# A gated block with quantized feed-forward: PSUM copies for the low weight halves, a second buffer for turned z, the down product three tiles behind, and tile norms on ScalarE

## The chip, the cores and the metric

One core of a Trainium2 chip runs the whole program as one launch. The metric is device time in microseconds; lower is better. The kernel before takes 396.05 us (median of 3 runs, 395.64 to 396.24).

## The reference

There are 2048 tokens (4 x 512) of width D = 512. Two gated residual branches follow one another:

```python
x = x + tanh(g_xattn) * experts(layernorm(x), token_ids)   # 4 experts, picked by token id
x = x + tanh(g_ffn)   * ffn(layernorm(x))
# expert e:  g = silu(h @ W[e].T); u = h @ W[e].T; y = (g * u) @ W[e].T    (all three weights are ctx[e])
# ffn:       out = bit_linear(silu(bit_linear(x, gate)) * bit_linear(x, val), out)   (hidden width 2048)
# bit_linear: each row of x scaled by 127 / max|x| and rounded, weights rounded to -1, 0, 1 times mean|w|
```

## The kernel before

**Experts.** The tokens are sorted by expert on the chip and cut into 19 units of 128 rows (`UNITS`), each with one expert. A unit is gathered from memory (`gather` on GpSimd), normalised on VectorE (`unit_stats`, `norm`), turned on TensorE (`turn_h`), and multiplied with its expert's 512 x 512 weight by 12 matmuls in half precision: high x high, low x high and high x low parts (`product`, L501). ScalarE and VectorE make g * u (`silu`, `gu`), TensorE turns that and multiplies again with the same weight, and VectorE adds the result to the rows (`x1`). GpSimd then writes the rows to `x1_rows` in memory (`scatter`). The low part of the weights (`w_low`) is made once in eight pieces of 128 x 1024, six on VectorE (L812) and two on GpSimd (L364), from the loaded weights and their high part, both in SBUF. One `slot` of TensorE handles the first product of unit j and the second of unit j - 1. Meanwhile ScalarE sums the feed-forward weights' magnitudes (`sum_abs`), GpSimd rounds them (`round_pair`, L375) and ScalarE makes them ternary (`sign_pair`).

**Feed-forward.** The rows come back as 16 tiles of 128 (`load_rows`). Per tile VectorE applies the norm (`tile_norm`, L914, into the PSUM bank `xn`; GpSimd makes the reciprocal deviation, `tile_rstd`, L341) and finds the row maximum (`x_max`, L920); ScalarE rounds (`x_round`, `x_unshift`); a DMA turns the tile (`turn_x`). TensorE does two halves of the gate product and of the value product, 8 matmuls of 512 columns each (`gate`, `val`), and the down product, 2 x 8 matmuls into one bank `o_ps` (`down`, L576). VectorE scales the four results and adds biases (`pre_gate` L940, `pre_val` L948). ScalarE takes silu (L730). GpSimd multiplies the halves to z (`z_pair`, L416, 128 x 1024). VectorE finds z's maximum (`z_max`, L953) and, after a few small steps, its scale (`z_scales`, L967); ScalarE rounds z in two halves (`z_round`, L718); GpSimd takes the rounding constant off the first half (`unshift_z`, L410) and ScalarE off the second (L726); SyncE's queue issues the turns (`turn_z`) into the single buffer `ziT`. VectorE ends a tile with `finish` (L978), and GpSimd stores it (`store`, L429) after it had added a bias to the residual rows (`add_bias`, L423).

**What sets the order.** Each engine's program is written out by hand, and runs strictly in that order; semaphores tie the engines. In feed-forward slot t VectorE runs `pre_gate(t,0)`, `pre_val(t,0)`, `z_max(t-1,1)`, `tile_norm(t+2)`, `x_max(t+2)` among the small steps of tile t-1's scale, `pre_gate(t,1)`, `z_max(t,0)`, `pre_val(t,1)`, `finish(t-2)`. GpSimd runs `z_pair(t-1,1)`, in every second slot `tile_rstd`, `store(t-3)`, `add_bias(t+1)`, `unshift_z(t-1)`, `z_pair(t,0)`. ScalarE runs `silu_gate(t,0)`, both `z_round(t-1)`, `unshift_z(t-1)`, `silu_gate(t,1)`, `x_round(t+2)`, `x_unshift(t+2)`. TensorE does tile t's four products with `down(t-2)` between them; each down product waits for the `finish` before it.

## Time and profile before

| | before |
|---|---|
| median of 3 runs | 396.05 us (395.64 to 396.24) |
| the profiled execution | 394.75 us, of which 393.0 us are the profile's span |
| TensorE matmul busy | 314.2 us (80%) |
| VectorE busy | 275.3 us (70%) |
| GpSimd busy | 230.3 us (59%) |
| ScalarE busy | 199.8 us (51%) |
| mean granted TensorE clock | 0.947 of full |

The busy times are sums over stages with different limits. Positions in the span are microseconds from its start. The experts' last product ends at about 157.3 us, and the first matmul of the feed-forward runs at 151.5 us. On VectorE and ScalarE rows that follow one another overlap by some 0.1 us, so steps are counted from start to start.

### The profile page before, as it was taken

The page shows a single profiled execution, that of the slowest core. Times are in us where ns is not written, and L with a number is a line of the kernel's source. Part 1 is how long each engine was busy: PE and PEld are TensorE (multiplying, and loading weights), DVE is VectorE, ACT ScalarE, POOL GpSimd, SP SyncE. Part 2 cuts the span into 40 slices and gives each one's busy share as a digit, 9 for nine tenths or more (in the row PEclk, how much of TensorE's full clock was granted, in tenths as well). Part 3 has the DMA queues.
Part 4 walks back from the last instruction along what each step waited for, and adds up shares of the span by engine and source line. Part 5 has one row for each costly group of instructions (what it writes and reads, how often), then busy time and mean ns, then how long its engine had stood idle before and what let it go on. Part 6 is the DMA issues. An engine that isn't in the chain of part 4 may idle for free.

```text
span 393.0 us, 5131 instructions
## 1 busy us (share of the span) xinstructions
PE 314.2 (80%) x1421; PEld 145.6 (37%) x1438; DVE 275.3 (70%) x519; ACT 199.8 (51%) x247; POOL 230.3 (59%) x237
## 2 busy tenths in 40 slices
PE   2966999999999599867598689787986986897533
PEld 1332555455555244323143234233432432343110
DVE  5696877678987476678668766966796687666510
ACT  4723558687864365163663456355536634555200
POOL 2564446877884933475656657575766566566310
PEclk9999999999999989999899899899899898999676
DMA  7697576652327411214432532344244314331240
...
DMA packets 54612, 47.50 MB, mean 121 GB/s; under 512 B 46847, under 2 KB 46847, under 8 KB 52288
## 3 DMA queue, kind: packets, MB, share of 16 engines
...
q8 instruction: 9, 0.15, 0.2%
q14 instruction: 11, 0.09, 0.1%
...
## 4 chain that ended last, share of the span: by engine, by line
POOL 36%; issue 25%; DVE 15%; PE 12%; DMA 8%; ACT 1%; POOLq 1%; DVEq 1%; SPq 1%
POOL w_both L416 15%; PE banks L501 8%; DMA xg<-in_x,gather_at 5%; DVE raw L948 5%; POOL raw L423 5%; POOL w_both L410 5%; POOL out L429 4%; POOL raw L375 2%; PE banks L576 1%; DVE x_sb L851 1%; POOL raw L341 1%; DVE bn L856 1%; POOL var_eps L338 1%; POOL xg L316 1%; DMA raw<-x_rows 1%
## 5 line engine op out<-in xcount | busy, mean ns | idle before, releaser
L501 PE MATMUL banks<-w_both,turned 128*128 x456 | 106.8, 384 | 7.2 <-DVE w_both L812 2.8
L576 PE MATMUL banks<-tern,w_both 128*128 128x512 bf16 x255 | 71.1, 432 | 43.1 <-DVE raw L978 34.1
L416 POOL TENSOR_TENSOR w_both<-raw 128x1024 f32<-128x1024 f32 (+1 forms) x32 | 74.9, 2340 | 41.4 <-DVE raw L948 41.4
L953 DVE TENSOR_REDUCE raw<-w_both 128x1 f32<-128x1024 f32 x32 | 38.9, 1216 | 55.8 <-POOL w_both L416 55.8
L556 PE MATMUL banks<-tern,raw 128*128 128x512 bf16 x241 | 62.5, 394 | 4.3 <-DVE raw L948 2.5
L501 PEld LDWEIGHTS banks<-w_both,turned 128*128 128x128 f16 x456 | 44.9, 98 | 56.1 <-issue 13.6
L718 ACT ACTIVATE w_both<-w_both,magic,raw 128x1024 f32 (+1 forms) x32 | 38.0, 1233 | 52.8 <-DVE raw L967 52.8
L565 PE MATMUL banks<-tern,raw 128*128 128x512 bf16 x256 | 60.5, 379 | 2.2 <-DVE raw L940 2.2
L730 ACT ACTIVATE raw<-raw 128x1024 f32<-128x1024 f32 x32 | 33.6, 1049 | 53.3 <-DVE raw L940 53.3
L576 PEld LDWEIGHTS banks<-tern,w_both 128*128 128x128 bf16 x256 | 26.3, 107 | 83.4 <-issue 39.9
L329 POOL DMA_INDIRECT x_rows<-x_sb,scatter_at x19 | 20.4, 1072 | 42.2 <-DVE x_sb L861 40.8
L940 DVE SCALAR_TENSOR_TENSOR raw<-banks,raw 128x1024 f32<-128x1024 f32 x32 | 40.9, 1277 | 0.5
L948 DVE SCALAR_TENSOR_TENSOR raw<-banks,raw 128x1024 f32<-128x1024 f32 x32 | 40.8, 1275 | 0.0
L556 PEld LDWEIGHTS banks<-tern,raw 128*128 (+1 forms) x256 | 26.1, 103 | 38.3 <-issue 7.7
L565 PEld LDWEIGHTS banks<-tern,raw 128*128 (+1 forms) x256 | 24.8, 98 | 33.2 <-DVE raw L940 3.7
L410 POOL TENSOR_SCALAR w_both<-w_both,magic,one 128x1024 bf16<-128x1024 f32 x15 | 17.9, 1192 | 31.8 <-ACT w_both L718 31.8
L670 ACT ACTIVATE tern<-raw,magic 128x1024 bf16<-128x1024 f32 x24 | 26.9, 1146 | 12.0 <-POOL raw L375 12.0
L375 POOL TENSOR_SCALAR raw<-raw,inv_gam,magic 128x1024 f32<-128x1024 f32 x24 | 28.8, 1202 | 0.1
L429 POOL DMA_INDIRECT out<-raw x16 | 17.0, 1063 | 18.9 <-DVE raw L978 16.5
...
L828 DVE BATCH_NORM_STATS2 bn<-xg 128x6 f32<-128x512 f32 x19 | 13.0, 686 | 17.1 <-DMA xg<-in_x,gather_at 17.1
L664 ACT ACTIVATE tern<-raw 128x1024 bf16<-128x1024 f32 x21 | 22.1, 1051 | 0.1
...
## 6 DMA issues: line engine op xcount, KB each, us to landing
...
w_both<-w_both SPq DMA_TRANSPOSE x32, 3.2
```

The lines of the kernel that those rows point to most:

```text
L375: nc.gpsimd.tensor_scalar(w, w, inv_gam[:, m:m + 1], magic[:, 0:1], ALU.mult, ALU.add).then_inc(rounded, 1)
L410: nc.gpsimd.tensor_scalar(zi[:, 0:H // 2], zq[:, 0:H // 2], magic[:, 1:2], one[:, 0:1], ALU.add, ALU.mult).then_inc(zi_made[0], 1)
L416: nc.gpsimd.tensor_tensor(z[:, t % 2, 2 * D * c:2 * D * c + width], g_sb[:, c, 0:width], v_sb[:, c, 0:width], ALU.mult).then_inc(z_made, 1)
L501: last = nc.tensor.matmul(acc[:, :], a[:, k * P:(k + 1) * P], flat(w[:, bass.ds(e4 + k, 1), :]), start=(k == 0 and i == 0), stop=(k == KD ...
L556: last = nc.tensor.matmul(ring[pair][:, b, :], flat(xiT[:, bass.ds(t % 2, 1), k, :]), tern[:, k * HC + 2 * c + b, :], start=(k == 0), stop ...
L565: last = nc.tensor.matmul(ring[pair][:, b, :], flat(xiT[:, bass.ds(t % 2, 1), k, :]), tern[:, G + k * HC + 2 * c + b, :], start=(k == 0), ...
L576: last = nc.tensor.matmul(o_ps, ziT[:, k, :], tern[:, 2 * G + k, :], start=(k == 0), stop=(k == G - 1))
L718: nc.scalar.activation(zq[:, a:b], flat(z[:, bass.ds(t % 2, 1), a:b]), ACT.Identity, scale=flat(sc[:, bass.ds(t, 1), 12:13]), bias=magic[: ...
L730: nc.scalar.activation(g_sb[:, c, :], g_sb[:, c, :], ACT.Silu).then_inc(s_made, 1)
L940: v.scalar_tensor_tensor(g_sb[:, c, :], flat(ring[(4 * t + 2 * c + 1) % 3 if t else 0]), col(t, 3), bias_g[:, 2 * c * D:2 * (c + 1) * D], ...
L948: v.scalar_tensor_tensor(v_sb[:, c, :], flat(ring[(4 * t + 2 * c + 2) % 3 if t else 1]), col(t, 4), bias_v[:, 2 * c * D:2 * (c + 1) * D], ...
L953: v.tensor_reduce(col(t, 5 + c), z[:, t % 2, 2 * D * c:2 * D * (c + 1)], AX.X, ALU.max, apply_absolute_value=True).then_inc(zmax_made, 1)
```

## The change

The kernel is changed in these places (all in one diff):

- Start: ScalarE copies six of the weight pieces, scaled, into PSUM (`w_copy`), and VectorE's `w_low` reads that copy instead of the SBUF tensor; two of these `w_low` run before the first unit's statistics. GpSimd's two `w_low` come after the next gather's issue and wait for a later `norm`. Unit 1 gets a second pair of turned-row buffers and its own bank for the first product, and is turned inside unit 0's product.
- Expert slots: the rounding and the signs of the last weights move later (four pairs into the feed-forward), four tiles instead of three are loaded early, and the first tile norms stand at the end of VectorE's slots.
- Feed-forward: GpSimd's `z_pair(t,0)` stands ahead of `unshift_z(t-1)`; ScalarE takes the first half's unshift and GpSimd the second's; `ziT` has two buffers (in the place of gathered rows); the down product and `finish` are three tiles behind; the norms of tiles 3 to 15 are one ScalarE instruction each, at the end of its slot (`norm`), whose shift GpSimd makes from mean and reciprocal deviation (`shift_of`); ten tiles' rows are held instead of eight, and the tokens of a tile are loaded later.

```diff
-    XR = 8
-    EARLY = 3
+    XR = 10
+    EARLY = 4
-    ROUNDED = (0, 0, 0, 0, 0, 0, 2, 4, 6, 8, 8, 10, 12, 14, 16, 18, 20, 22, 24)
-    SIGNED = (0, 0, 0, 0, 0, 0, 1, 3, 5, 7, 8, 9, 11, 13, 15, 17, 19, 22, 24)
+    ROUNDED = (0, 0, 0, 0, 0, 0, 2, 4, 6, 8, 8, 10, 12, 14, 16, 18, 20, 20, 20, 22, 24)
+    SIGNED = (0, 0, 0, 0, 0, 0, 1, 3, 5, 7, 8, 9, 11, 13, 15, 17, 19, 20, 20)
...
-        hT_hi, hT_lo, guT_hi, guT_lo = (turned[:, i, :] for i in range(4))
+        hTs = [(turned[:, 0, :], turned[:, 1, :]), tuple(tern[:, 2 * G + i, :].bitcast(f16) for i in (4, 5))]
+        guT_hi, guT_lo = turned[:, 2, :], turned[:, 3, :]
...
-        x_frees = 6
+        x1_in = area(XR * ROW).rearrange("p (b d) -> p b d", b=XR)
+        x_frees = 4
-        y_out = area(2 * D).rearrange("p (b d) -> p b d", b=2)
+        y_out = xg[:, 4:6, :]
...
-        ziT = area(H // 2, bf16).rearrange("p (h m) -> p h m", m=P)
+        ziT = xg[:, 0:4, :].rearrange("p a b -> p (a b)").bitcast(bf16).rearrange("p (b h m) -> p b h m", b=2, m=P)
...
+        w_pair = [banks[:, 4:6, :], banks[:, 2:4, :], banks[:, 6:8, :], banks[:, 4:6, :],
+                  banks[:, 4:6, :], banks[:, 6:8, :]]
...
-                if t >= 1:
-                    sp.wait_ge(z_read[half], t)
-                sp.dma_start_transpose(ziT[:, half * G // 2:(half + 1) * G // 2, :],
+                if t == 0:
+                    sp.wait_ge(x1_made, UNITS)
+                if t >= 2:
+                    sp.wait_ge(z_read[half], t - 1)
+                sp.dma_start_transpose(ziT[:, t % 2, half * G // 2:(half + 1) * G // 2, :],
                                        zi[:, half * H // 2:(half + 1) * H // 2]).then_inc(z_turned[half], 16)
...
-            for t in range(EARLY, XT):
-                load_rows(t)
-                load_tokens(t)
+            load_rows(XT)
             for t in range(TILES + 1):
-                if t + XT < TILES:
-                    load_rows(t + XT)
-                if 3 <= t < TILES - 1:
-                    load_tokens(t + 1)
+                if t + XT + 1 < TILES:
+                    load_rows(t + XT + 1)
                 if t >= 1:
                     turn_z(t - 1, 0)
                     turn_z(t - 1, 1)
                 if t + 2 < TILES:
                     turn_x(t + 2)
+                if XT <= t < TILES:
+                    load_tokens(t)
...
-                for p in rounds[:1]:
+                rounds = range(ROUNDED[j - 1], ROUNDED[j]) if j >= 1 else range(0)
+                early_rounds = 1 if j < UNITS else 0
+                for p in rounds[:early_rounds]:
                     round_pair(p)
+                if j == UNITS + 1:
+                    pool.wait_ge(y_done, UNITS)
+                    z_pair(0, 0)
                 if j >= 2:
                     scatter(j - 2)
...
+                if j < 2:
+
+                    pool.wait_ge(h_made, j + 3)
+                    w_low(LOW_DVE + j)
                 if j + 3 < UNITS:
                     unit_rstd(j + 3)
...
+                if j == UNITS + 1:
+                    z_pair(0, 1)
+                for p in rounds[early_rounds:]:
                     round_pair(p)
 
...
-                pool.wait_ge(zq_made[0], t + 1)
+                pool.wait_ge(zq_made[1], t + 1)
                 if t >= 1:
-                    pool.wait_ge(z_turned[0], 16 * t)
-                nc.gpsimd.tensor_scalar(zi[:, 0:H // 2], zq[:, 0:H // 2], magic[:, 1:2], one[:, 0:1],
-                                        ALU.add, ALU.mult).then_inc(zi_made[0], 1)
+                    pool.wait_ge(z_turned[1], 16 * t)
+                nc.gpsimd.tensor_scalar(zi[:, H // 2:H], zq[:, H // 2:H], magic[:, 1:2], one[:, 0:1],
+                                        ALU.add, ALU.mult).then_inc(zi_made[1], 1)
...
+            def shift_of(t):
+
+                pool.wait_ge(tile_rstds, rstd_groups(t))
+                of = x1_in[:, t % XR, :]
+                nc.gpsimd.tensor_scalar(of[:, MEAN:MEAN + 1], of[:, MEAN:MEAN + 1], of[:, RSTD:RSTD + 1], -1.0,
+                                        ALU.mult, ALU.mult).then_inc(shifts, 1)
...
             for t in range(TILES):
-                if t >= 1:
+                if t >= 2:
                     z_pair(t - 1, 1)
-                if t == 1:
-                    tile_rstd(3, 1)
-                if t >= 2 and t % 2 == 0 and t + 3 < TILES:
-                    tile_rstd(t + 2, 2)
-                if t >= 3:
-                    store(t - 3)
+                if t == 0:
+                    shift_of(3)
+                if t >= 4:
+                    store(t - 4)
                 if t == 1:
                     pool.wait_ge(bias_scaled, 1)
-                    add_bias(0)
-                    add_bias(1)
-                if 1 <= t < TILES - 1:
-                    add_bias(t + 1)
                 if t >= 1:
+                    add_bias(t - 1)
+                if t >= 1:
+                    z_pair(t, 0)
                     unshift_z(t - 1)
-                z_pair(t, 0)
+                if t % 2 == 0 and t + 4 < TILES:
+                    tile_rstd(t + 4, 2)
+                    shift_of(t + 4)
+                    shift_of(t + 5)
             z_pair(TILES - 1, 1, D)
-            for t in range(TILES - 3, TILES):
+            add_bias(TILES - 1)
+            for t in range(TILES - 4, TILES):
                 store(t)
 
...
+                first = isinstance(j, int) and j == 1
+                if first:
+                    pe.wait_ge(wlo_made, 3)
+                if before and not first:
                     turn_gu(j - 1)
...
+                if first:
+                    turn_gu(j - 1)
...
+            def turn_second():
+                pe.wait_ge(hTlo_made, 1)
+                turn_h(1)
+
+            slot(0, before=False, after=False, between=turn_second)
...
-                    down(t - 2, 0, start_down)
+                    down(t - 3, 0, start_down)
                 if downs:
-                    down(t - 2, 1)
+                    down(t - 3, 1)
...
+            ffn_slot(2, 0, downs=False)
+            ffn_slot(3, 1, start_down=True)
-            for t in range(TILES - 3, TILES):
+                    ffn_slot(3 * r + n + 4, (n + 2) % 3)
+            ffn_slot(TILES - 3, 2)
+            ffn_slot(TILES - 2, 0)
+            ffn_slot(TILES - 1, 1, downs=False)
+            for t in range(TILES - 4, TILES):
                 down(t, 0)
                 down(t, 1)
...
+            w_high(0)
+            w_high(1)
+            w_copy(0)
+            w_high(2)
+            w_high(3)
+            w_copy(1)
+            w_high(4)
+            w_high(5)
+            w_copy(3)
+            w_high(6)
+            w_copy(2)
+            w_high(7)
...
+            def norm(t):
+                act.wait_ge(shifts, t - 2)
+                act.wait_ge(xq_made, t)
+                of = flat(x1_in[:, bass.ds(t % XR, 1), :])
+                nc.scalar.activation(xn, of[:, 0:D], ACT.Identity, scale=of[:, RSTD:RSTD + 1],
+                                     bias=of[:, MEAN:MEAN + 1]).then_inc(xn_made, 1)
...
-            def ffn_slot(t, before=True, start=False, after=True):
+            def ffn_slot(t, before=True, start=False, after=True, ahead=True):
                 silu_gate(t, 0)
                 if before:
                     z_round(t - 1, 0, start)
+                    unshift_z(t - 1, start)
                     z_round(t - 1, 1, start)
-                    unshift_z(t - 1, start)
...
+                if ahead:
+                    norm(t + 3)
...
-            ffn_slot(0, before=False)
+            silu_gate(0, 0)
+            x_round(2)
+            x_unshift(2)
+            sign_pair(20)
+            sign_pair(21)
+            silu_gate(0, 1)
+            norm(3)
+            sign_pair(22)
+            sign_pair(23)
...
-                v.scalar_tensor_tensor(flat(w_lo[:, 2 * p:2 * p + 2, :]), flat(raw[:, 2 * G + 2 * p:2 * G + 2 * p + 2, :]), W_SCALE,
+                dve.wait_ge(w_copied, COPIED[p])
+                v.scalar_tensor_tensor(flat(w_lo[:, 2 * p:2 * p + 2, :]), flat(w_pair[p]), 1.0,
                                        flat(w_hi[:, 2 * p:2 * p + 2, :]), ALU.mult, ALU.subtract).then_inc(wlo_made, 1)
...
+            w_low(0)
+            w_low(1)
             padding_before()
-            scatter_places()
             unit_stats(0)
             norm(0)
             unit_stats(1)
-            w_low(0)
+            scatter_places()
             h_low(0)
             norm(1)
-            w_low(1)
+            w_low(2)
+            h_low(1)
+            w_low(3)
             unit_stats(2)
             dve.wait_ge(tanh_made, 1)
             v.tensor_scalar(y_scale[:, :], tanh_g[:, 0:1], 1 / (GU_SCALE * W_SCALE), None, ALU.mult).then_inc(yscale_made, 1)
-            w_low(2)
...
-                if j == EARLY_SLOT + 1:
-                    x_max(0)
-                    x_gamma(0)
-                if j >= EARLY_SLOT + 2:
-                    if j == EARLY_SLOT + 2:
-                        tile_norm(1)
-                        x_max(1)
-                        x_gamma(1)
-                        x_scales(1)
-                if j == 0:
-                    w_low(3)
-                    unit_stats(3)
                 if j == 1:
-                    w_low(4)
+                    w_low(5)
+                if j == 2:
+                    unit_stats(5)
                 if DVE_SUM <= j < DVE_SUM + PAIRS - ACT_SUMS:
                     sum_abs(ACT_SUMS + j - DVE_SUM)
...
+                if j > EARLY_SLOT:
+                    tile_norm(j - EARLY_SLOT - 1)
+                    x_max(j - EARLY_SLOT - 1)
...
-                if 1 <= t < TILES - 2:
-                    tile_norm(t + 2)
...
                 if t == 0:
-                    tile_norm(2)
-                    x_max(2)
-                    x_gamma(2)
-                    x_scales(2)
-                if 2 <= t < TILES - 1:
-                    finish(t - 2)
+                    z_max(t, 0)
+                if 3 <= t < TILES - 1:
+                    finish(t - 3)
...
-            finish(t - 2)
...
-            finish(t - 1)
+            finish(t - 3)
...
+            finish(t - 2)
+            finish(t - 1)
             finish(t)
```

## Rows read from the trace of the kernel before

**Rows 1.** Stretches: core's us, then each engine's busy (instructions), clock, DMA

```profile
21.00:41.50 20.50, 14.05 (x70) 7.12 (x71) 16.67 (x26) 6.98 (x14) 9.64 (x12) 1.00 0.88 326
41.50:131.10 89.60, 88.50 (x466) 47.68 (x464) 68.91 (x136) 59.61 (x95) 63.08 (x88) 1.00 0.54 183
131.10:157.30 26.20, 20.70 (x92) 9.73 (x93) 18.13 (x33) 15.36 (x20) 13.38 (x16) 0.93 0.15 46
```

**Rows 2.** Timeline of GpSimd over one feed-forward slot

```profile
255.22 1.20 POOL L410 TENSOR_SCALAR w_both<-w_both,magic,one 128x1024 bf16<-128x1024 f32 x1 [2.53 <-ACT w_both L718]
256.38 2.37 POOL L416 TENSOR_TENSOR w_both<-raw 128x1024 f32<-128x1024 f32 x1
261.34 2.36 POOL L416 TENSOR_TENSOR w_both<-raw 128x1024 f32<-128x1024 f32 x1 [2.59 <-DVE raw L948]
...
263.93 0.72 POOL L341 TENSOR_TENSOR raw<-var_eps,halves 128x2 f32<-128x2 f32 x1
264.85 1.08 POOL L429 DMA_INDIRECT out<-raw  x1 [0.20 <-issue]
265.96 1.10 POOL L423 TENSOR_TENSOR raw<-raw 128x512 f32<-128x512 f32 x1
268.74 1.19 POOL L410 TENSOR_SCALAR w_both<-w_both,magic,one 128x1024 bf16<-128x1024 f32 x1 [1.68 <-ACT w_both L718]
```

**Rows 3.** Timeline of VectorE over one feed-forward slot

```profile
250.63 1.21 DVE L953 TENSOR_REDUCE raw<-w_both 128x1 f32<-128x1024 f32 x1
251.76 0.81 DVE L914 TENSOR_SCALAR banks<-raw 128x512 f32<-128x512 f32 x1
...
252.79 0.68 DVE L920 TENSOR_REDUCE raw<-banks 128x1 f32<-128x512 f32 x1
...
258.78 1.22 DVE L953 TENSOR_REDUCE raw<-w_both 128x1 f32<-128x1024 f32 x1 [3.38 <-POOL w_both L416]
259.92 1.27 DVE L948 SCALAR_TENSOR_TENSOR raw<-banks,raw 128x1024 f32<-128x1024 f32 x1
```

**Rows 4.** Timeline of ScalarE: the rounding of tiles 1, 6 and 14

```profile
186.35 2.37 ACT L718 ACTIVATE w_both<-w_both,magic,raw 128x1024 f32 x2 [3.53 <-DVE raw L967]
...
253.87 2.37 ACT L718 ACTIVATE w_both<-w_both,magic,raw 128x1024 f32 x2 [3.26 <-DVE raw L967]
256.28 1.15 ACT L726 ACTIVATE w_both<-w_both,magic 128x1024 bf16<-128x1024 f32 x1
...
258.28 0.76 ACT L703 ACTIVATE raw<-banks,magic,raw 128x512 f32<-128x512 f32 x1
...
359.25 2.37 ACT L718 ACTIVATE w_both<-w_both,magic,raw 128x1024 f32<-128x1024 f32 x2 [1.90 <-DVE raw L967]
```

**Rows 5.** Timeline of TensorE: two half products inside the feed-forward, two downs at its end

```profile
255.35 1.89 PE L576 MATMUL banks<-tern,w_both 128*128 128x512 bf16 x8
257.07 1.89 PE L556 MATMUL banks<-tern,raw 128*128 128x512 bf16 x8
...
368.15 5.38 PE L576 MATMUL banks<-tern,w_both 128*128 128x512 bf16 x16 [6.48 <-DVE raw L978]
379.91 6.33 PE L576 MATMUL banks<-tern,w_both 128*128 128x512 bf16 x16 [6.37 <-DMA w_both<-w_both]
```

**Rows 6.** Timeline of GpSimd and VectorE at the start, idle time before in brackets

```profile
19.17 1.06 POOL L338 TENSOR_TENSOR var_eps<-mean_var,halves 128x1 f32<-128x1 f32 x1
...
29.69 0.18 POOL L338 TENSOR_TENSOR var_eps<-mean_var,halves 128x1 f32<-128x1 f32 x1 [1.16 <-DVE mean_var L832]
...
33.59 0.69 DVE L828 BATCH_NORM_STATS2 bn<-xg 128x6 f32<-128x512 f32 x1 [3.41 <-DMA xg<-in_x,gather_at]
```

**Rows 7.** Timeline of VectorE, the first tile norm

```profile
131.31 0.81 DVE L914 TENSOR_SCALAR banks<-raw 128x512 f32<-128x512 f32 x1 [3.90 <-POOL raw L341]
```

**Rows 8.** Costliest groups of the page: rounding and sign of weights

```profile
L670 ACT ACTIVATE tern<-raw,magic 128x1024 bf16<-128x1024 f32 x24 | 26.9, 1146 | 12.0 <-POOL raw L375 12.0
L375 POOL TENSOR_SCALAR raw<-raw,inv_gam,magic 128x1024 f32<-128x1024 f32 x24 | 28.8, 1202 | 0.1
```

171 lines of the change are left out of this document (95 added, 76 removed).

## The prediction

> **What bounds the kernel now.** I read the stretches first, then the chain of waits, then the timelines of the engines over one feed-forward slot. In the experts' stage TensorE is busy 88.5 of 89.6 us at clock 1.00 [rows 1], so little is to be had there. Around it lie two stages with holes: from 21 to 41.5 us it is busy 14.05 of 20.5 us, and from 131.1 to 157.3 us 20.7 of 26.2 us at clock 0.93. The rest, 236 us, is the feed-forward, where the two GpSimd rows of the same line stand 268.74 - 255.22 = 13.52 us apart: one tile [rows 2].
>
> TensorE is not what sets that pitch. Eight matmuls start 257.07 - 255.35 = 1.72 us before the next eight [rows 5], and a tile has six such groups: 10.35 us. No engine is full; a ring through three of them is. Reading it off [rows 2 to 4]: ScalarE starts rounding z of tile t-1 at 253.87; GpSimd takes off the constant at 255.22 and only then makes the first half of tile t's z at 256.38; VectorE has idled 3.38 us for it and takes its maximum at 258.78, then the value step behind it at 259.92; GpSimd, which idled 2.59 us, makes the second half at 261.34; VectorE's next maximum comes 0.45 us after that is done, and from maximum to the next rounding it is 253.87 - 250.63 = 3.24 us. That is 7.47 + 2.81 + 3.24 = 13.52. The reader is to see the crossing: z of a new tile stands in GpSimd's queue behind the unshift of the old one.
>
> **The steady feed-forward.** The change puts `z_pair(t,0)` ahead of `unshift_z(t-1)`, so the ring is cut and two shorter paths remain. I count from D, the start of `z_max` of a tile's second half.
>
> Path A, by the scale. From maximum to rounding 3.24 us less the tile norm's 0.81 - 0.09 = 0.72, which leaves VectorE: 2.52. On ScalarE two roundings and now an unshift between them: 2.37 + 1.15 less the overlaps, 3.5. GpSimd unshifts the second half, 1.2. In even slots up to t = 10 it then makes two tiles' deviations and two shifts: 0.2 + 0.72 + two new [128 x 1] operations. These are not in the trace. The nearest rows are 0.18 for a [128 x 1] addition and 0.72 for the power [rows 6, 2]; I take 0.25, as they are a product; so 1.45 together (1.3 to 2.4). Then `z_pair(t,1)`, 2.4. Sum: 2.52 + 3.5 + 1.2 + 2.4 = 9.65 us in an odd slot, 11.1 in an even one.
>
> Path B, by the queues of GpSimd and VectorE. From D, when GpSimd has just ended a z: store with its gap 1.28, bias 1.17 (1.10 here), z of the first half 2.4; on VectorE maximum 1.14, value step 1.19, `finish` 0.66, then the next tile's gate and value steps, 1.2 each. The last four differ from rows only by the overlap of 0.09 [rows 3]; `finish` is a half-width form of the value step, which I take at its half plus a little. Sum 10.2 us.
>
> So even slots take 11.1 and the others 10.2, both paths near TensorE's 10.35. From the scale of tile 1 to that of tile 14 there are 13 slots, five of them even with deviations: 5 x 11.1 + 8 x 10.2 = 137.1, less 0.6 as tile 14 has no `x_max` behind it: **136.5 us**. Now it is 359.25 - 186.35 = 172.9 us [rows 4]. TensorE's own floor is 13 x 10.35 = 134.5, so it runs close behind without setting the pace. `down(t-3)` finds its turned z one slot old, and its wait for `finish` of the tile before ends about 2 us early; the second buffer of `ziT` covers the turns, which wait for `down(t-3)`. If that cover were gone each tile would wait for a turn, some 4 us.
>
> The norm on ScalarE has no row. The nearest is the rounding of a tile from PSUM, 0.76 us of the same width [rows 4]; the bounds are 0.6 and 1.15, the unshift's. I take 0.76. ScalarE then has 2 x 1.04 + 2.37 + 1.15 + 0.76 + 0.72 + 0.76 = 7.9 us in a slot of 10.5. The norm stands last in its slot, about 3 us ahead of the `x_max` that reads it, so it costs nothing; without this lead its 0.76 would enter path A. SyncE's order (rows of tile t+5, turns of z and x, tokens of t) holds no wait that ends late: the tokens wait for `store(t-4)`, issued at the slot's start.
>
> **The start.** The trace has 6.45 us of TensorE idle time between 21 and 41.5 us [rows 1]. VectorE waits 3.41 us for unit 4's rows [rows 6], whose gather is queued on GpSimd behind a `w_low` of 2.1 us and behind unit 2's deviation. Now the gather comes first (-1.4 us), and unit 1's first product no longer waits for two `w_low`, since two are made before unit 0's rows have landed. I walked the queues piece by piece with these durations: the second product of unit 1 starts at 34.7 instead of 41.2 us. I take **6.0 us** (bounds 0, if the six new ScalarE copies of about 1 us each delay the turns, and 6.9).
>
> One step of it stands on little: the [128 x 1] addition takes 1.06 us beside a `w_low` of VectorE and 0.18 elsewhere [rows 6]. I count it at 0.2, as VectorE now reads PSUM; two such on the way to the gather are 1.8 us. The Trainium skill (SBUF — State Buffer, "Who interferes with whom") says that a VectorE instruction with two SBUF inputs contends with a GpSimd instruction that reads SBUF; the trace agrees as far as 1.06 beside 0.18 us goes. By it the 1.8 us go; if it did not hold here the term would be 4.2.
>
> **Into the feed-forward.** From 131.1 to 157.3 us TensorE is busy 20.7 of 26.2 us at clock 0.93 [rows 1]: 5.5 us idle and 0.07 x 26.2 = 1.8 us lost to the clock, 7.3 together. VectorE waited 3.90 us for the first tile norm's deviation [rows 7] with `gu` behind it, and the clock fell after that. The norm now stands last in the slot, behind `gu`. Of the 7.3 us I take **6.6**, as `gu_low` still waits behind a norm for some tenths (bounds 3 and 7.3).
>
> Then, from the experts' end (Y) to the scale of tile 1, now 186.35 - 157.3 = 29.05 us. New: second value step of tile 0 done at Y + 4.8, z 7.2, two roundings of weights on GpSimd 9.6 and a shift 9.9, norm of tile 3 on ScalarE 10.6, two signs 12.8 [rows 8], silu 13.8, z 16.2, maximum 17.4, value step 18.6, second z 21.0, scale **23.3 us**. A stall is moved here, not only removed: the last signs stand ahead of tile 1's silu. Gain 5.75 us.
>
> **The end.** From the scale of tile 14 to the end it is now 393.0 - 359.25 = 33.75 us. New: the scale of tile 15 at +9.1; `finish(12)` to 9.9; then three times down and finish, the first down at a lower clock. The rows show 5.38 and 6.33 us for 16 matmuls after 6.5 us of idle time [rows 5], against 3.45. So 15.5, 16.2, 20.4, 24.7, and store and end 6.0 more (379.91 + 6.33 to 393.0 is 6.8, with a finish of 0.75): **30.5 us**. Gain 3.2.
>
> **Sum.** Experts' end 157.3 - 6.0 - 6.6 = 144.7; + 23.3 + 136.5 + 30.5 = 335.0 us of span, where it is 393.0. With the 1.75 us around the span 336.8; the median of the runs lies 1.3 above the profiled execution: **338 us**. A difference under 0.2% is what a measurement here can't tell from none.
>
> **Rivals.** (1) The paths are longer than counted, because a wait over three engines ends later than its parts: a pitch of 11.3 instead of 10.5, thus + 10 us: 348 us. For it: both paths run within 1 us of one another and of TensorE, so delays of one pass to the others. Against: the slack of 2 to 3 us at `finish` and the norm. 24%. (2) The start and the entry give only the lower bounds, 3 instead of 12.6 us, with the feed-forward as counted: 348 us, too. The fixed order could turn out with a new head-of-queue wait, as signs ahead of silu. 10%. (3) TensorE sets the pace and the small operations are hidden: 134.5 for 136.5, and the upper bounds 7.3 and 6.9: 3.6 us less, about 334 us. 10%. (4) The change does not cut the ring: `z_pair` still ends after the old tile's rounding, as ScalarE's two silu stand around the roundings. Then the pitch stays 13.5 less the norm's 0.7, and 338 + 13 x 2.3 = 368 us. 4%. (5) Slower than before: TensorE at its lower level (1.2 GHz) over the feed-forward, after its short waits in each slot. Each tile would then take 20.7 us; it decides when more than 58 / 10.35 = 5.6 of the 13 tiles are wholly at the low level. Against it: idle gaps of under 1 us left the clock at 1.00 in the experts' stage [rows 1]. 2%. My forecast, 331 to 343, holds 50%.
>
> The likeliest case's own range is 331 to 343. To leave out no more than two in ten I take 330 to 353, which holds (1), (2) and (3). Faster 0.97, same 0.01, slower 0.02.
>
> **What would show it.** The pitch of `z_pair(t,0)`: 10.2 and 11.1 us in turn; GpSimd idle before its unshift only, not before z; TensorE busy above 95% in the slots; VectorE idle under 1 us a slot; ScalarE's norm 0.7 to 0.8 us and 2 us or more ahead of `x_max`. The second product of unit 1 at 35 us, the experts' end at 145, the GpSimd additions at the start 0.2 us. Wrong it goes if the pitch is over 11, if TensorE's rows show the long form inside the slots, or if `h_hi` of the first units comes late behind the copies.

## The result, and the profile after

The changed kernel takes 343.23 us (median of 4 runs, 342.64 to 343.98) beside 395.85 us of the kernel before on the same chip: a ratio of 0.8677, 95% interval 0.865 to 0.8704. The profiled execution took 343.1 us, with a span of 341.4. The forecast was 338 us with 330 to 353: the result lies inside that range and just above the likeliest case's own 343, 5.2 us above the point.

| position in the span, us | before | forecast | after |
|---|---|---|---|
| second product of unit 1 starts | 41.23 | 34.7 | 34.92 |
| experts' last product ends | 157.3 | 144.7 | 149.7 |
| scale of tile 1 (its rounding starts) | 186.35 | 168.0 | 173.87 |
| scale of tile 14 | 359.25 | 304.5 | 311.05 |
| end | 393.0 | 335.0 | 341.4 |

In the lines of the changed kernel `product` is L533, `turn_gu` L540, `gu_hi` L718, `gu_low` L935, `sign` L733, `round_pair` L393, `gather` L334, `scatter` L347; in the feed-forward `z_pair` L398, GpSimd's unshift L441, ScalarE's L804, `z_round` L789, silu L808, `norm` L796, `shift_of` L454, `pre_gate` L1033, `pre_val` L1041, `z_max` L1046, `finish` L1073, `down` L618. The kernels of the experiments differ by a few lines.

Stretches of the profile after, with the columns of [rows 1]:

```profile
21.00:41.50 20.50, 19.18 (x102) 10.23 (x101) 17.43 (x31) 11.91 (x20) 11.68 (x16) 1.00 0.89 338
41.50:125.00 83.50, 81.23 (x423) 43.65 (x422) 64.13 (x129) 58.47 (x93) 57.13 (x77) 0.98 0.53 170
125.00:151.00 26.00, 22.05 (x110) 10.90 (x110) 19.56 (x42) 12.77 (x19) 13.67 (x19) 1.00 0.39 131
151.00:175.00 24.00, 19.01 (x79) 7.97 (x80) 19.05 (x33) 15.21 (x16) 20.59 (x17) 0.93 0.34 78
175.00:295.00 120.00, 114.58 (x520) 51.50 (x528) 103.68 (x179) 85.39 (x92) 95.16 (x75) 1.00 0.45 101
295.00:341.40 46.40, 31.85 (x138) 13.63 (x138) 24.99 (x35) 15.39 (x15) 23.79 (x17) 0.92 0.34 81
```

TensorE is now busy 19.18 of 20.5 us at the start where it was 14.05, and 95.5% of the time in the slots. Beside 5.4 us spread over the slots and 2.3 us in the experts' stage (2.06 of them in the first new stall, below), idle time is left in three places: 3.95 us from 125 to 151, 5 us behind that, and 14.6 us at the end. One sign of the prediction did not come: VectorE is idle 16.3 of the 120 us, some 1.5 us a slot and not under 1.

**The slots.** Timelines of ScalarE, GpSimd, VectorE and TensorE after, over one odd and one even slot, which answer to [rows 2 to 5]:

```profile
228.09 1.24 ACT L789 ACTIVATE w_both<-w_both,magic,raw 128x1024 f32 x1 [3.85 <-DVE raw L1060]
238.35 1.24 ACT L789 ACTIVATE w_both<-w_both,magic,raw 128x1024 f32 x1 [2.67 <-DVE raw L1060]
249.78 1.24 ACT L789 ACTIVATE w_both<-w_both,magic,raw 128x1024 f32 x1 [3.85 <-DVE raw L1060]
...
242.02 1.19 POOL L441 TENSOR_SCALAR w_both<-w_both,magic,one 128x1024 bf16<-128x1024 f32 x1 [2.07 <-ACT w_both L789]
243.44 0.72 POOL L359 TENSOR_TENSOR raw<-var_eps,halves 128x2 f32<-128x2 f32 x1
244.27 0.49 POOL L454 TENSOR_SCALAR raw<-raw 128x1 f32<-128x1 f32 x2
244.72 2.36 POOL L398 TENSOR_TENSOR w_both<-raw 128x1024 f32<-128x1024 f32 x1
...
235.70 1.21 DVE L1046 TENSOR_REDUCE raw<-w_both 128x1 f32<-128x1024 f32 x1
247.12 1.22 DVE L1046 TENSOR_REDUCE raw<-w_both 128x1 f32<-128x1024 f32 x1 [1.57 <-POOL w_both L398]
...
233.69 1.90 PE L618 MATMUL banks<-tern,xg 128*128 128x512 bf16 x8 [0.77 <-DMA xg<-w_both]
```

From scale to scale it is 10.26 us in the odd slot and 11.43 in the even one, forecast as 10.2 and 11.1. Path A can be read off for the even slot: maximum to rounding 238.35 - 235.70 = 2.65, two roundings with an unshift between them 242.02 - 238.35 = 3.67, unshift 1.15, deviations and shifts 1.55, z 2.40: 11.42. The odd slot is path B: from one maximum of a second half to the next, 225.43 to 235.70, the chain runs through GpSimd's store, bias and first z and then VectorE's five steps, as counted. The norm on ScalarE takes 0.76 us in a slot, as taken.

**The first new stall.** Timelines of GpSimd, VectorE and TensorE after, 37 to 51 us:

```profile
37.62 1.07 POOL L347 DMA_INDIRECT x_rows<-x_sb,scatter_at  x1 [0.90 <-issue]
39.00 0.99 POOL L334 DMA_INDIRECT xg<-in_x,gather_at  x1 [0.31 <-DVE x_sb L941]
...
44.25 0.69 DVE L918 BATCH_NORM_STATS2 bn<-xg 128x6 f32<-128x512 f32 x1 [4.10 <-DMA xg<-in_x,gather_at]
...
45.79 0.65 PE L540 MATMUL banks<-ident,gu_sb 128*128 128x128 f32 x4 [2.06 <-DVE gu_sb L930]
46.55 4.45 PE L533 MATMUL banks<-w_both,turned 128*128 x12
```

Unit 6's gather is issued behind the first scatter, and its rows come 5.25 us after the issue, where the median of the 19 gathers is 4.3. VectorE, which is to take its statistics, stands still 4.10 us, with `gu` behind it. TensorE waits 2.06 us, and the product after the wait takes 4.45 instead of 2.75 us (the window's clock is 0.98).

**The second.** Timelines of GpSimd, ScalarE, VectorE and TensorE after, 125 to 137 us, where [rows 7] had the wait of before:

```profile
125.82 1.09 POOL L347 DMA_INDIRECT x_rows<-x_sb,scatter_at  x1 [6.77 <-issue]
129.26 2.37 POOL L393 TENSOR_SCALAR raw<-raw,inv_gam,magic 128x1024 f32<-128x1024 f32 x2
...
130.48 2.33 ACT L733 ACTIVATE tern<-raw,magic 128x1024 bf16<-128x1024 f32 x2 [4.92 <-POOL raw L393]
132.72 0.58 ACT L718 ACTIVATE turned<-banks 128x512 f16<-128x512 f32 x1
...
129.68 0.80 DVE L1007 TENSOR_SCALAR banks<-raw 128x512 f32<-128x512 f32 x1
133.33 0.69 DVE L935 SCALAR_TENSOR_TENSOR turned<-banks,turned 128x512 f16<-128x512 f32 x1 [2.13 <-ACT turned L718]
...
134.16 2.76 PE L533 MATMUL banks<-w_both,turned 128*128 x12 [3.23 <-DVE turned L935]
```

The tile norm (L1007) no longer waits. But TensorE still does, 3.23 us: for `gu_low`, which waits for ScalarE's `gu_hi`, which stands behind two signs, which wait for roundings, which GpSimd makes behind a late scatter (by the code it waits for the rows of the four early tiles). Here the clock did not fall: behind the wait of 3.23 us the product takes 2.76 us.

**The end.** Timelines of VectorE and TensorE after, which answer to [rows 5]:

```profile
319.56 0.75 DVE L1073 SCALAR_TENSOR_TENSOR xg<-banks,raw 128x512 f32<-128x512 f32 x1
...
311.22 3.62 PE L618 MATMUL banks<-tern,xg 128*128 128x512 bf16 x16
320.46 2.72 PE L618 MATMUL banks<-tern,xg 128*128 128x512 bf16 x6 [5.62 <-DVE xg L1073]
323.40 2.12 PE L618 MATMUL banks<-tern,xg 128*128 128x512 bf16 x9 [0.22 <-issue]
326.46 3.61 PE L618 MATMUL banks<-tern,xg 128*128 128x512 bf16 x16 [0.93 <-DVE xg L1073]
```

Down(12) ends at 314.8, but its `finish` runs at 319.56, behind everything for the last tile's scale; down(13) waits 5.62 us for it and then takes 5.1 us for 16 matmuls instead of 3.6.

### The profile page after: what moved, and what is told of

The parts are those of the page before. It is cut to its first block, busy times and chain, and to the rows that moved or that the text cites. A ratio compares the mean times of both kernels' runs of the same rounds, so it can differ in the third digit from the quotient of the medians.

```text
span 341.4 us, 5309 instructions
## 1 busy us (share of the span) xinstructions
PE 299.8 (88%) x1423; PEld 143.7 (42%) x1438; DVE 263.8 (77%) x506; ACT 213.7 (63%) x266; POOL 230.3 (67%) x248
## 4 chain that ended last, share of the span: by engine, by line
PE 32%; POOL 24%; issue 13%; DVE 13%; DMA 8%; ACT 6%; SPq 1%; POOLq 1%; ACTq 1%; DVEq 0%
PE banks L533 14%; POOL w_both L398 10%; PE banks L618 6%; ACT w_both L789 4%; POOL raw L393 4%; DMA xg<-w_both 4%; PE banks L607 3%; PE banks L598 3%; POOL w_both L441 3%; DVE raw L1046 3%; PE banks L510 2%; POOL raw L448 2%; DMA xg<-in_x,gather_at 2%; PE banks L515 1%; PE banks L540 1%
## 5 line engine op out<-in xcount | busy, mean ns | idle before, releaser
L533 PE MATMUL banks<-w_both,turned 128*128 x444 | 103.8, 384 | 6.8 <-DVE turned L935 5.1
L398 POOL TENSOR_TENSOR w_both<-raw 128x1024 f32<-128x1024 f32 (+1 forms) x32 | 75.0, 2343 | 1.7 <-ACT raw L808 1.3
L618 PE MATMUL banks<-tern,xg 128*128 128x512 bf16 x248 | 60.7, 385 | 12.8 <-DVE xg L1073 9.5
L789 ACT ACTIVATE w_both<-w_both,magic,raw 128x1024 f32 (+1 forms) x32 | 39.4, 1233 | 44.8 <-DVE raw L1060 44.8
L533 PEld LDWEIGHTS banks<-w_both,turned 128*128 128x128 f16 x444 | 43.8, 99 | 53.5 <-issue 11.5
L598 PE MATMUL banks<-tern,raw 128*128 128x512 bf16 x251 | 60.5, 382 | 4.1 <-DVE raw L1041 3.9
L607 PE MATMUL banks<-tern,raw 128*128 128x512 bf16 x255 | 61.2, 383 | 1.3 <-DVE raw L1033 1.1
L1046 DVE TENSOR_REDUCE raw<-w_both 128x1 f32<-128x1024 f32 x32 | 38.9, 1216 | 20.9 <-POOL w_both L398 20.9
L618 PEld LDWEIGHTS banks<-tern,xg 128*128 (+1 forms) x256 | 25.1, 99 | 45.3 <-issue 18.5
L347 POOL DMA_INDIRECT x_rows<-x_sb,scatter_at x19 | 20.4, 1073 | 34.1 <-DVE x_sb L951 22.6
L1041 DVE SCALAR_TENSOR_TENSOR raw<-banks,raw 128x1024 f32<-128x1024 f32 x32 | 40.8, 1276 | 0.8 <-PE banks L607 0.8
L1033 DVE SCALAR_TENSOR_TENSOR raw<-banks,raw 128x1024 f32<-128x1024 f32 x32 | 40.8, 1275 | 0.5 <-PE banks L598 0.3
L808 ACT ACTIVATE raw<-raw 128x1024 f32<-128x1024 f32 x32 | 33.4, 1044 | 7.1 <-DVE raw L1033 7.1
L441 POOL TENSOR_SCALAR w_both<-w_both,magic,one 128x1024 bf16<-128x1024 f32 x15 | 17.8, 1189 | 26.9 <-ACT w_both L789 26.9
L733 ACT ACTIVATE tern<-raw,magic 128x1024 bf16<-128x1024 f32 x24 | 26.7, 1144 | 7.0 <-POOL raw L393 6.9
L334 POOL DMA_INDIRECT xg<-in_x,gather_at x19 | 19.4, 1019 | 14.1 <-DVE gather_at L891 9.0
L393 POOL TENSOR_SCALAR raw<-raw,inv_gam,magic 128x1024 f32<-128x1024 f32 x24 | 28.4, 1186 | 0.0
L461 POOL DMA_INDIRECT out<-xg,raw x16 | 16.8, 1050 | 15.8 <-DVE xg L1073 13.9
L714 ACT ACTIVATE gu_sb<-banks 128x512 f32<-128x512 f32 x19 | 11.3, 594 | 18.4 <-PE banks L533 18.4
```

The lines of the kernel that those rows point to most:

```text
L393: nc.gpsimd.tensor_scalar(w, w, inv_gam[:, m:m + 1], magic[:, 0:1], ALU.mult, ALU.add).then_inc(rounded, 1)
L398: nc.gpsimd.tensor_tensor(z[:, t % 2, 2 * D * c:2 * D * c + width], g_sb[:, c, 0:width], v_sb[:, c, 0:width], ALU.mult).then_inc(z_made, 1)
L441: nc.gpsimd.tensor_scalar(zi[:, H // 2:H], zq[:, H // 2:H], magic[:, 1:2], one[:, 0:1], ALU.add, ALU.mult).then_inc(zi_made[1], 1)
L533: last = nc.tensor.matmul(acc[:, :], a[:, k * P:(k + 1) * P], flat(w[:, bass.ds(e4 + k, 1), :]), start=(k == 0 and i == 0), stop=(k == KD ...
L598: last = nc.tensor.matmul(ring[pair][:, b, :], flat(xiT[:, bass.ds(t % 2, 1), k, :]), tern[:, k * HC + 2 * c + b, :], start=(k == 0), stop ...
L607: last = nc.tensor.matmul(ring[pair][:, b, :], flat(xiT[:, bass.ds(t % 2, 1), k, :]), tern[:, G + k * HC + 2 * c + b, :], start=(k == 0), ...
```

## The experiments

Medians, ratios to the kernel before and 95% intervals; the positions come from each kernel's profiled execution.

| kernel | us | ratio (interval) | last product starts | scale 1 to 14 | scale 14 to end |
|---|---|---|---|---|---|
| after | 343.23 | 0.8677 (0.865 to 0.8704) | 147.11 | 137.2 | 30.4 |
| swap_alone | 353.46 | 0.893 (0.8875 to 0.8985) | 156.91 | 139.2 | 29.6 |
| no_swap | 412.74 | 1.0437 (1.0377 to 1.0498) | 149.53 | 195.7 | 36.0 |
| one_buffer | 427.35 | 1.0812 (1.074 to 1.0884) | 149.27 | 210.1 | 40.4 |
| norm_dve | 349.38 | 0.883 (0.8778 to 0.8883) | 148.78 | 142.7 | 31.4 |
| low_from_sbuf | 346.87 | 0.8773 (0.8728 to 0.8818) | 149.37 | 137.6 | 31.8 |
| signs_later | 342.98 | 0.8666 (0.8626 to 0.8705) | 144.76 | 137.1 | 31.2 |
| gather_first | 343.30 | 0.8678 (0.8636 to 0.872) | 145.97 | 137.1 | 31.6 |
| both | 339.38 | 0.858 (0.854 to 0.8621) | 144.00 | 137.2 | 30.3 |
| roles_back | 334.59 | 0.8462 (0.8422 to 0.8501) | 143.05 | 132.0 | 31.5 |
| entry | 338.92 | 0.8574 (0.8534 to 0.8614) | 143.25 | 137.2 | 30.5 |
| all_three | 333.85 | 0.8437 (0.84 to 0.8474) | 144.66 | 132.1 | 31.6 |
| early_finish | 327.14 | 0.8263 (0.8228 to 0.8298) | 145.15 | 131.6 | 24.2 |

**swap_alone: the order alone.** The kernel before, with one line moved:

```diff
+                z_pair(t, 0)
                 if t >= 1:
                     unshift_z(t - 1)
-                z_pair(t, 0)
```

> The kernel before with one move only: GpSimd makes the first half of tile t's z ahead of the unshift of tile t-1. If the order on GpSimd alone cut the ring, the pitch falls from 13.5 to about 10.8 us although norm, single buffer and the down product two tiles behind stay, and the time is about 362 us (358 to 368). If the second buffer, the larger lag or the norm on ScalarE is needed as well, the pitch stays above 12.5 us and the time above 380 us.

353.46 us: 42 of the 52.6 us, more than expected. The 13 slots take 139.2 us, 10.71 each, in turn about 10.5 and 10.9. This one move brings all but 2.0 us of what the whole change brings in the slots. The rest of the change gives 9.8 us before the experts' last product, 2.0 us from there to the scale of tile 1, and takes 0.8 at the end. These are profiled executions, and they lie further apart (13.1 us) than the medians (10.2): in swap_alone's, the experts' last product starts 2.2 us later than in that of the kernel before (156.91 and 154.71), from the same code.

**no_swap: all but the order.** The changed kernel with `z_pair(t, 0)` behind `unshift_z(t - 1)`.

> The changed kernel with only that order undone: the unshift stands ahead of the first half of the next tile's z. By the ring as I read it the second half's unshift now waits for two roundings and an unshift (3.5 us), so the ring is 3.5 + 1.2 + 2.4 + 2.6 + 2.4 + 2.5 = 14.6 us, and the time about 395 us, as long as the kernel before. If buffers and lag carry the gain, it stays near 350 us.

412.74 us, slower than before and than expected. Timelines of ScalarE, GpSimd and VectorE of this kernel:

```profile
241.38 1.24 ACT L789 ACTIVATE w_both<-w_both,magic,raw 128x1024 f32 x1 [2.67 <-DVE raw L1060]
256.60 1.24 ACT L789 ACTIVATE w_both<-w_both,magic,raw 128x1024 f32 x1 [2.67 <-DVE raw L1060]
...
245.04 1.19 POOL L441 TENSOR_SCALAR w_both<-w_both,magic,one 128x1024 bf16<-128x1024 f32 x1 [4.25 <-ACT w_both L789]
...
248.57 1.22 DVE L1046 TENSOR_REDUCE raw<-w_both 128x1 f32<-128x1024 f32 x1 [5.87 <-POOL w_both L398]
```

The ring is back, at 15.22 us a tile. In the kernel before GpSimd's unshift came 255.22 - 253.87 = 1.35 us behind the scale [rows 2, 4]; here it is 3.66, since GpSimd now has the second half and waits for both roundings and ScalarE's unshift. 13.52 + 2.31 less the norm's 0.7 is 15.1. So the exchange of the unshifts lengthens the ring by itself, and without the new order the rest of the change costs 17 us.

**one_buffer: the cover taken away.** Turns also wait for the down product of the tile just before:

```diff
-                if t >= 2:
-                    sp.wait_ge(z_read[half], t - 1)
+                if t >= 1:
+                    sp.wait_ge(z_read[half], t)
```

> The changed kernel in which the turn of a z half also waits for the down product of the tile just before it, as with a single buffer; down and finish stay three tiles behind. By my statement that each tile would wait some 4 us or more for a turn, since the turn of x is queued behind the turn of z, the pitch is 14.5 to 16.5 us and the time 395 to 420 us. If the slack of a slot covers the wait, it stays at 343 us.

427.35 us, beyond the upper end. Timelines of SyncE's queue and TensorE of this kernel:

```profile
265.08 6.41 SPq L277 DMA_TRANSPOSE xg<-w_both  x2
271.58 1.22 SPq L269 DMA_TRANSPOSE raw<-raw  x1
282.38 6.41 SPq L277 DMA_TRANSPOSE xg<-w_both  x2
...
274.39 3.59 PE L598 MATMUL banks<-tern,raw 128*128 128x512 bf16 x8 [4.21 <-DMA raw<-raw]
277.77 2.80 PE L607 MATMUL banks<-tern,raw 128*128 128x512 bf16 x8
```

A tile takes 282.38 - 265.08 = 17.30 us, some 6.6 more than after. The wait came as forecast: the turn of the next tile's x stands behind the z turns in the same queue, and the gate product waits 4.21 us for it. What the "some 4 us" left out is what comes behind it: the next two groups of matmuls take 3.59 and 2.80 us instead of 1.89, and last 2.6 us longer together. 10.35 + 4.2 + 2.6 is 17.1.

**norm_dve: the norms back on VectorE**, from the same shifts, ahead of the small steps of the scale.

> The changed kernel with the norms of tiles 3 to 15 back on VectorE, at the place they had before, from the same shifts. If the path by the scale sets the even slots (0.7 us longer) and the path by the queues the others, 5 x 0.7 + 8 x 0.2 = 5 us are added: 348 us. If TensorE or GpSimd hides it, 343 us. If VectorE's queue is full, all 13 slots get 0.7 us: 352 us.

349.38 us: the 13 slots take 142.7 instead of 137.2 us, 5.5 more, and the norm lies on the way to the scale. From the maximum (239.75) to the rounding (243.09) it takes 3.34 us where after has 2.65. The five even slots are 0.68 us longer each and the other eight 0.27 on average, close to the 0.7 and 0.2 expected.

**low_from_sbuf: no PSUM copies.** `w_copy` is left out and `w_low` reads the SBUF tensor, in the new order.

> The changed kernel without the six ScalarE copies: VectorE's low parts are made from the SBUF tensor again, in the changed order. If an instruction of VectorE with two SBUF inputs holds up GpSimd, the 128 x 1 addition beside such an instruction at about 30 us takes 1.0 us instead of 0.2 and the low parts of both engines get in each other's way; the experts' part ends 1 to 2 us later: 344.5 us. If the copies only load ScalarE, the time is the same or up to 1 us shorter.

346.87 us, 3.6 more than after. At the start the price is higher: the second product of unit 1 starts at 39.30 instead of 34.92 us. Timelines of GpSimd and VectorE of this kernel:

```profile
12.19 3.23 POOL L334 DMA_INDIRECT xg<-in_x,gather_at  x1 [8.96 <-DVE gather_at L883]
...
33.68 1.08 POOL L356 TENSOR_TENSOR var_eps<-mean_var,halves 128x1 f32<-128x1 f32 x1 [0.87 <-DVE mean_var L913]
...
12.05 2.34 DVE L893 SCALAR_TENSOR_TENSOR w_both<-raw,w_both 128x1024 f16<-128x1024 f32 x2
33.52 1.19 DVE L893 SCALAR_TENSOR_TENSOR w_both<-raw,w_both 128x1024 f16<-128x1024 f32 x1
```

The long addition of [rows 6] is back at one place (1.08 us beside `w_low`). But the larger part is one that I had not thought of: the issue of the first gather takes 3.23 us beside two `w_low` from SBUF. With `w_low` from PSUM, at the same time, it takes 1.15. Unit 0's statistics start 2.06 us later for it. Of the other 2.3 us, 1.5 lie in unit 0's product: TensorE had waited 2.39 us before it, its clock is 0.83 from 21 to 31 us, and four matmuls take 1.89 us instead of 1.03. 0.9 lie in the stretch of the long addition.

**signs_later: the second stall's first suspect.** Two signs leave the slot of unit 16:

```diff
-    SIGNED = (0, 0, 0, 0, 0, 0, 1, 3, 5, 7, 8, 9, 11, 13, 15, 17, 19, 20, 20)
+    SIGNED = (0, 0, 0, 0, 0, 0, 1, 3, 5, 7, 8, 9, 11, 13, 15, 17, 17, 20, 20)
```

> The changed kernel with ScalarE's signs of weight pairs 17 and 18 moved from slot 16 to slot 17. In the trace ScalarE idles 4.9 us before them, for roundings that GpSimd has queued behind the row loads of four tiles, and the high part of unit 16's turned product stands behind them; TensorE idles 3.2 us. If that is the cause, the stall goes: 3 us less, about 340 us. If the first tile norm on VectorE is (as I had it), nothing changes: 343 us.

Timelines of ScalarE and TensorE of this kernel:

```profile
133.72 3.21 ACT L733 ACTIVATE tern<-raw,magic 128x1024 bf16<-128x1024 f32 x3
...
130.82 2.76 PE L533 MATMUL banks<-w_both,turned 128*128 x12 [0.23 <-DVE turned L935]
138.28 2.76 PE L533 MATMUL banks<-w_both,turned 128*128 x12 [1.66 <-DVE turned L935]
```

The wait of 3.23 us falls to 0.23, with the tile norm where it was: the signs were its cause. The three signs that now stand in the next slot cost a wait of 1.66 us there, where after has 0.67. The profiles of all these kernels agree. From the first product of unit 17 to the last product of all it takes 17.35 to 17.52 us in the six kernels whose signs are moved, and 17.98 to 22.02 in the six that have them where after has them (after 19.37). So the stall's length varies, and the move takes off 0.5 to 4.7 us. The last product starts 2.35 us earlier. The median moves by only 0.25 us, within what this measurement can tell, though this profiled execution is 1.5 us shorter.

**gather_first: the first stall's suspect.** Unit 6's gather is issued ahead of the first scatter:

```diff
+                if j == 2:
+                    gather(j + 4)
                 if j >= 2:
                     scatter(j - 2)
-                if j + 4 < UNITS:
+                if j != 2 and j + 4 < UNITS:
                     gather(j + 4)
```

> The changed kernel with GpSimd's gather of unit 6 ahead of the scatter of unit 0. In the trace VectorE waits 4.1 us for unit 6's rows, TensorE 2.1 us, and its next product runs at the lower clock (4.45 instead of 2.75 us). If the place in GpSimd's queue is the cause, the rows come 1.4 to 2 us earlier and 2 to 3.5 us are gained: 340.5 us. If the load of the memory channels by the weights is, the rows land when they do now: 343 us.

The long product of 4.45 us is gone, but the median is unchanged. In this execution the second product of unit 1 starts at 36.57 us, since the clock rose later (0.92 instead of 1.00 from 21 to 41.5 us); from there to the product behind unit 6's it is 2.9 us shorter, and 1.5 of them come back in small waits until the first product of unit 17. The profile of norm_dve has the same late clock and no such long product either, without this move, and one_buffer has none with the early clock. So the long product is not the gather's alone.

What the move is worth shows over all profiles: from the second product of unit 1 to the first of unit 17 it takes 90.6 to 91.6 us in the six kernels with it and 91.6 to 93.6 in the five without it and with `w_copy`, 1.5 us less on average. The stall is shortened and not removed: in both the gather is issued 1.94 us earlier (37.06), the rows land 5.8 us behind it, and VectorE still waits 2.52 us. Whether the load of the memory by the weights makes them so late was not tested.

**both: the two repairs together.**

> Both moves together: signs of pairs 17 and 18 a slot later and unit 6's gather first. If both causes are right and the gains add: 337.5 us. If one stall takes the place of the other: 340 us.

339.38 us, 3.85 less than after. The experts' last product starts 3.1 us earlier. That this is nearly the sum of the two (2.35 + 1.14) is luck: gather_first came to unit 17 0.25 us later than after, and had its 1.14 from a shorter second stall (17.98 for 19.37 us). Why neither shows in a median alone lies partly at the end: from the scale of tile 14 to the end it takes 31.2 and 31.6 us in the two, 30.3 in both, with the same instructions and the same waits. From the start of down(13), behind its 5.6 us wait, to that of down(14) it is 6.0 us in after, 6.9 and 7.25 in these two, and 5.9 in both: the products behind the wait take their long form for a longer or a shorter while. That this explains the medians, too, was not seen in their own runs and stays a guess.

**roles_back: the exchange of the unshifts undone** in the kernel of both repairs: GpSimd again takes the first half, ScalarE the second, behind both roundings.

> The kernel of both repairs, with the two unshifts given back as the kernel before had them: GpSimd takes the constant off the first half, ScalarE off the second half, behind both roundings; all else stays. The theory that path A, by the scale, sets the even slots (11.42 us from scale to scale against some 10.05 in the odd ones, while each of GpSimd's other steps fits into 10.3): GpSimd's unshift and the two tiles' deviations (1.15 + 1.55 us) now run while ScalarE is still at its roundings and its silu, so the second z starts when silu is done, some 1.3 us earlier in an even slot. Even slots then fall to the next limit, TensorE's 10.35 us, and the 13 slots from the scale of tile 1 to that of tile 14 take some 134.5 instead of 137.2 us: about 336.7 us where both repairs have 339.4. The rival, that the queues of GpSimd and VectorE set every slot and the roles do not matter: still 137 us for the 13 slots and 339.4 us. A second rival, that handing the later half to ScalarE makes its turn and the down product late: pitch above 10.6 in all slots and 340 us or more.

334.59 us, 4.8 less, where 2.7 were expected. Timelines of ScalarE and GpSimd, and a stretch of this kernel:

```profile
230.04 2.37 ACT L791 ACTIVATE w_both<-w_both,magic,raw 128x1024 f32 x2 [2.78 <-DVE raw L1062]
240.41 2.37 ACT L791 ACTIVATE w_both<-w_both,magic,raw 128x1024 f32 x2 [2.79 <-DVE raw L1062]
...
234.63 2.37 POOL L398 TENSOR_TENSOR w_both<-raw 128x1024 f32<-128x1024 f32 x1 [0.48 <-ACT raw L810]
...
175.00:295.00 120.00, 119.53 (x548) 54.41 (x556) 109.46 (x185) 87.97 (x95) 101.31 (x75) 1.00 0.48 106
```

GpSimd unshifts while ScalarE rounds the second half, and the second z waits 0.48 us for silu alone. Slots take 10.36 us, odd and even alike: TensorE is busy 119.53 of 120 us. Here TensorE sets the pace, as in rival (3). The 13 slots take 132.0 us, less than the 134.5 of that floor: the first two take 9.65 us each, as TensorE has no down product to do before slot 3, and four others are 0.3 to 0.5 us short of the pace. The end is 1.2 us longer than in both, and the last product starts 1.0 us earlier.

**entry: two moves behind the experts.** In the kernel of both repairs GpSimd makes tile 3's shift ahead of the last two roundings, and ScalarE makes the last two pairs of signs behind its work of slot 1.

> The kernel of both repairs with two moves at the entry of the feed-forward: GpSimd makes tile 3's shift ahead of the last two roundings of weights instead of behind them, and ScalarE makes the last two pairs of signs behind its work of slot 1 instead of ahead of silu of tile 1. In the trace of both repairs the norm of tile 3 waits 5.94 us for that shift (156.83), and VectorE's maximum of tile 3, with the scale of tile 0 right behind it, waits 1.05 us for the norm. Theory, that this wait sets the entry: the scale of tile 0 and all behind it come 1.0 us earlier, the scale of tile 1 lies 25.8 instead of 26.8 us behind the start of the experts' last product, and the time is 338.4 us where both repairs have 339.4. If instead the signs ahead of silu were the whole of it, as my prediction had it, the gain would be their 2.1 us: 337.3 us. If GpSimd's queue (roundings, deviations, bias) sets the first z of tile 1 on its own: nothing, 339.4 us.

From the last product's start to the scale of tile 1 it takes 25.48 instead of 26.78 us, 1.3 us less. Timelines of GpSimd, the first z of tile 1, in after and in this kernel:

```profile
163.84 2.36 POOL L398 TENSOR_TENSOR w_both<-raw 128x1024 f32<-128x1024 f32 x1 [1.34 <-ACT raw L808]
...
158.70 2.35 POOL L398 TENSOR_TENSOR w_both<-raw 128x1024 f32<-128x1024 f32 x1
```

In after this z waits 1.34 us (in both 1.29) for silu of tile 1. Here it waits for nothing and follows GpSimd's own bias step. So the gain is that wait: neither the 1.0 us of the maximum behind the norm nor the whole 2.1 us of the signs. Behind silu's delay stand the shift, the norm and the signs in one row, and as both moves are in one kernel, the run does not tell their shares. The median falls by 0.46 us, which the intervals do not tell from none.

**all_three: both repairs, the roles and the entry.**

> Both repairs, the roles of the unshifts given back and the entry's moves together. If each works on its own stretch and they add up: 1.0 us from the entry and 2.7 us from the 13 slots, about 335.7 us where both repairs have 339.4. If TensorE sets the pace once the even slots are short, the slots cannot go under 134.5 us, and a faster entry only brings that limit sooner: between 335.7 and 336.7 us. It would be the fastest of these kernels in either case; if the roles do not matter it stays at 338.4 us.

333.85 us, 0.74 less than without the entry's moves, which the intervals do not tell from none either; the way to the scale of tile 1 is 25.40 us here, too.

**early_finish: VectorE's order at the end.**

```diff
             t, last = TILES - 1, slice(D, 2 * D)
+            finish(t - 3)
             dve.wait_ge(s_made, 2 * TILES)
...
             z_scales(t)
-            finish(t - 3)
+            finish(t - 2)
             for half in range(2):
...
-            finish(t - 2)
             finish(t - 1)
```

> The kernel of all three with VectorE's order changed after the last slot: finish of tile 12 stands ahead of the last tile's small z step instead of behind the scale of tile 15, and finish of tile 13 directly behind that scale. In the trace of all three TensorE ends down(12) at 305.9 us and then waits 5.46 us for that finish; down(13), whose clock drops after the wait, lasts from 311.38 to 317.85, the turns of tile 15 into the buffer that down(13) reads are issued at 315.03, and down(14) and down(15) follow at 318.79 and 323.33; the span ends 6.7 us behind the start of the last finish, at 333.7. Theory, that this one place in VectorE's queue sets the end: down(13) starts at 306.8 and ends at 310.4, finish(13) runs at 310.5, down(14) from 311.4 to 315.0, and down(15) starts at 316, at once behind finish(14), since the turns of tile 15 are then issued when it is rounded (312.5) and have landed by 315.5. The last finish starts at 319.7 and the span ends at 326.5: 7 us less, 327 us in the median where all three have 333.85. Rival: the scale of tile 15 and its turns set the end (rounded at 312.5, turned some 3 us later, one down, one finish), with little left to gain because the earlier finish delays the scale: 331 us or more. Second rival, no change: TensorE's low clock after any wait costs what the order saves, 333.8 us.

327.14 us, as worked out. Timelines of VectorE, TensorE and SyncE's queue of this kernel:

```profile
305.98 0.75 DVE L1076 SCALAR_TENSOR_TENSOR xg<-banks,raw 128x512 f32<-128x512 f32 x1 [0.17 <-PE banks L620]
...
306.87 3.61 PE L620 MATMUL banks<-tern,xg 128*128 128x512 bf16 x15 [0.94 <-DVE xg L1076]
311.42 3.61 PE L620 MATMUL banks<-tern,xg 128*128 128x512 bf16 x16 [0.94 <-DVE xg L1076]
315.97 3.61 PE L620 MATMUL banks<-tern,xg 128*128 128x512 bf16 x16 [0.94 <-DMA xg<-w_both]
...
312.49 2.73 SPq L277 DMA_TRANSPOSE xg<-w_both  x2
```

Finish(12) runs at 305.98, directly behind down(12). TensorE's waits between the last four down products are 0.94 us each, the turns of tile 15 are issued when they are ready (312.49 instead of 315.03), and none of the last four down products shows the long form. From the scale of tile 14 to the end it takes 24.2 us.

## Why the prediction came out as it did

- **The ring and its cut: right.** swap_alone and no_swap show that the order of `z_pair` and the unshift carries the change. The paths left were the two that I counted, as the rows show: 10.26 and 11.43 us for 10.2 and 11.1. The 13 slots took 137.2 us (136.5 forecast), and part of that closeness is luck: the five even slots took 57.1 us for 55.5, the other eight 80.1 for 81.0. Rival (1), a pitch of 11.3, did not come.
- **Experts' end, 144.7 us: wrong by 5.0 of the 6.4 us that the span was missed by (341.4 for 335.0).** The start's term of 6.0 was right (6.3 measured). The entry's 6.6 was mis-sized: it brought 3.95 us, the lead over the kernel before being 3.65 us at the second product of unit 15 and 7.6 at the last product. The wait for the tile norm had gone, and behind it stood another, of signs behind late roundings. From the first product of unit 17 to the last product it is 19.37 us after, and signs_later takes 2.0 us of it. I had named VectorE's wait [rows 7] as the cause and not asked what else hangs on the same late GpSimd queue. And the gain of the start did not last: 4.2 us went at unit 6's rows, and only 1.6 came back until unit 15, where the kernel before had small waits of its own. A faster start used the rows up faster, while their gather stood behind a scatter.
- **The median: a lucky term.** I added 1.3 us for the median over the profiled execution; it lies 0.1 us over it. So the point was missed by 5.2 us and not by 6.4.
- **Scale of tile 1, 23.3 us behind the experts' end: 24.2.** The moved stall came step by step as counted: roundings, shift, norm, two signs, silu, z. The first z of tile 1 ended 16.5 us behind the experts' end for 16.2 forecast. What I had not asked is what the row costs: 1.3 us, as GpSimd's own queue is the next limit (entry).
- **Unshift of the first half on ScalarE: missed as a cost.** I put it into path A as 3.5 us for roundings and unshift, and did not ask whether path A would be shorter without the exchange. It would: 4.8 us of time (roles_back).
- **The end, 30.5 us: 30.4.** Right as a sum (its own last step, 24.7 + 6.0, is 30.7; measured are 24.4 + 6.0), but the order behind it was taken as given. early_finish shows that 6.7 us of it (333.85 to 327.14) were one place in VectorE's queue.
- **The second buffer as cover: right, its price too low** (one_buffer: 6.6 us a tile, not 4; the wait was 4.2, the rest the longer matmuls behind it).
- **PSUM copies: right, for a wider reason.** The Trainium skill (SBUF — State Buffer, "Who interferes with whom") says that a VectorE instruction with two SBUF inputs contends with a GpSimd instruction that reads SBUF. The additions agree (1.08 beside 0.19 to 0.25 us). The section calls the shared ports an exclusive lock. The gather's issue, which began 0.14 us behind two `w_low` of 2.34 us together, agrees: it took 2.08 us more. By my count 1.8 us of the start hung on the copies; in low_from_sbuf it is 4.4. The same section infers, of tensor_tensor, that two SBUF inputs do not hold up the making of descriptors; this run speaks against carrying that over to `w_low`, and the measurement decides.
